# The residual as transposes at the head of an output projection's accumulation

## The reference

```python
x0  = adapter(x, cond)                      # low-rank, relu, plus x itself
h   = rmsnorm(x0) * norm1
q, k, v = split(h @ qkv_w + qkv_b)          # 16 heads, 4 key/value heads, 64 wide
q, k = rope(q), rope(k)
y   = attention(q, k, v, sink)              # causal, inside a sequence of 64
x2  = x0 + y @ proj_w + proj_b              # the residual and the output projection
h2  = rmsnorm(x2) * norm2
e, g = top4(h2 @ gate_w + gate_b)           # 4 of 32 experts, softmax of the four
out = x + x2 + sum_e g_e * (silu(h2 @ Wg_e) * (h2 @ Wu_e)) @ Wd_e
```

## Time and profile before

| what | value |
|---|---|
| median of three runs | 1031.28 us |
| lowest and highest run | 1029.86 and 1033.35 us |
| span of the profiled execution | 1031.5 us |
| its own time | the profile gives none beside the span |
| PE busy | 898.5 us, 87% |
| PE weight loads busy | 738.7 us, 72% |
| VectorE busy | 805.3 us, 78% |
| ScalarE busy | 512.2 us, 50% |
| GpSimd busy | 552.1 us, 54% |
| chain that ended last, PE's share | 49% |

### The profile page before, as it was taken

One profiled execution on the slowest core, in us unless ns is written; L12 is line 12 of the kernel. 1 busy time (PEld: TensorE's weight loads), 2 busy tenths in 40 slices (PEclk: granted clock), 3 DMA queues, 4 the chain that ended last, 5 costly groups with the idle time before them and its releaser, 6 DMA issues.

```text
span 1031.5 us, 21542 instructions
## 1 busy us (share of the span) xinstructions
PE 898.5 (87%) x7336; PEld 738.7 (72%) x7336; DVE 805.3 (78%) x1877; ACT 512.2 (50%) x1193; POOL 552.1 (54%) x513
## 2 busy tenths in 40 slices
PE   3859998988899989988871399999999999999986
PEld 1537676776677767766750288888888888888874
DVE  3878799988978898988857177777777777777787
ACT  1224362735437363453752266666666666566631
POOL 2436466877768688696768133333433344333340
PEclk9869999999999999999995599999999999999998
DMA  7235869687696977959875897778678758663599
GB/s 224 57 93 181 268 218 268 224 275 250 232 290 214 295 241 252 293 192 301 289 252 202 325 307 266 264 243 309 224 254 273 265 186 308 223 226 103 179 365 340
DMA packets 127684, 251.95 MB, mean 244 GB/s; under 512 B 18706, under 2 KB 66327, under 8 KB 127002
## 3 DMA queue, kind: packets, MB, share of 16 engines
q1 hardware_dynamic: 83866, 187.59, 55.4%
q0 software_dynamic: 13872, 34.64, 9.2%
q10 hardware_dynamic: 29840, 28.34, 9.0%
HBM read 136.19 MB, written 102.66 MB: 232 GB/s over the span
## 4 chain that ended last, share of the span: by engine, by line
PE 49%; POOL 14%; DMA 11%; DVE 10%; issue 7%; SPq 4%; ACT 3%; ACTq 0%; DVEq 0%; POOLq 0%
PE scores L970 10%; PE gbank L970 10%; POOL lists L672 10%; PE scores L989 5%; PE gbank L989 5%; DMA w_parts<-ring 4%; PE gbank L761 3%; DMA ring<-in_W_up 3%; POOL ring L679 3%; PE gbank L838 3%; DMA rows_in<-lists 3%; DVE ring L1401 2%; PE gbank L944 2%; PE scores L944 2%; PE gbank L979 2%
## 5 line engine op out<-in xcount | busy, mean ns | idle before, releaser
L694 POOL DMA_INDIRECT pick_rows<-rows_out,pair_i x161 | 160.9, 999 | 269.4 <-ACT rows_out L1232 260.7
L679 POOL TENSOR_TENSOR ring<-ring 128x512 fp32r<-128x512 f32 x96 | 122.6, 1291 | 47.0 <-ACT ring L1167 46.5
L970 PE MATMUL scores<-ring,in_part 128*128 x486 | 134.7, 412 | 0.0
L970 PE MATMUL gbank<-ring,in_part 128*128 x480 | 131.8, 409 | 0.0
L672 POOL DMA_INDIRECT lists<-put_rows,slot_i x104 | 103.4, 994 | 47.5 <-issue 28.0
L838 PE MATMUL gbank<-w_o,ring 128*128 128x256 f32 x512 | 123.2, 396 | 6.0 <-ACT ring L1113 6.0
L761 PE MATMUL gbank<-h_t,w_qk 128*128 128x512 f32 x480 | 122.1, 407 | 6.7 <-DVE h_t L1388 5.0
L1401 DVE SCALAR_TENSOR_TENSOR ring<-gbank,b_qk,rope 128x512 f32<-128x512 f32 x160 | 109.9, 745 | 16.6 <-PE gbank L761 16.0
L838 PEld LDWEIGHTS gbank<-w_o,ring 128*128 128x128 f32 x512 | 99.8, 199 | 26.0 <-ACT ring L1113 9.7
L761 PEld LDWEIGHTS gbank<-h_t,w_qk 128*128 128x128 f32 x480 | 89.7, 192 | 31.5 <-issue 8.6
L1167 ACT ACTIVATE ring<-ring 128x512 fp32r<-128x512 f32 x96 | 59.9, 628 | 90.8 <-DMA w_parts<-ring 50.9
(11 more groups left out here) (200 smaller groups left out, 1899.0 us busy)
## 6 DMA issues: line engine op xcount, KB each, us to landing
w_parts<-ring SPq DMA_DIRECT2D x192, 256.0 KB, 3.2
ring<-w_parts SPq DMA_DIRECT2D x32, 1536.0 KB, 7.9
rows_in<-lists ACTq DMA_DIRECT2D x161, 136.0 KB, 3.8
ring<-in_W_up SPq DMA_DIRECT2D x64, 256.0 KB, 4.0
picks<-pick_rows SPq DMA_DIRECT2D x8, 2048.0 KB, 12.8
ring<-in_W_down SPq DMA_DIRECT2D x32, 256.0 KB, 4.2
q_r<-rot SPq DMA_DIRECT2D x16, 512.0 KB, 6.9
q_r<-ring SPq DMA_DIRECT2D x16, 512.0 KB
```

The source lines that it names most:

```text
L679: e.tensor_tensor(lower, lower.bitcast(F32), upper.bitcast(F32), ALU.subtract).then_inc(s_lower, 1)
L694: e.indirect_dma_start(out=pick_rows, out_offset=bass.IndirectOffsetOnAxis(ap=pair_i[:, i:i + 1], axis=0), in_=rows_out[i % NY][:, :], in_ ...
L970: ins = e.matmul(front[i % FRONTS], in_parts[i % IN_BUFS][x][:, c, :], ring[:, bass.ds(at + y * WE + c * 2 * DFF, 2 * DFF)], start=k == 0, ...
```

## The change

The two blocks of the residual become transposes (`is_transpose`) and move ahead of the output products. The first of them begins the bank; the second and the eight products only add to it or write where nothing has been written. The wait for `x0_t` and the take of the bank come first, the wait for `y_t` moves behind the transposes, and the last product raises `s_proj`. Beside that, `plan_wait` becomes a table of 16-bit numbers.

```diff
+U16 = mybir.dt.uint16
...
-    plan_wait = sb("plan_wait", [1, 2 * P], I32)
+    plan_wait = sb("plan_wait", [1, 2 * P], U16)
...
         def project(t, banks):
             m, s = divmod(t, TPM)
-            w.wait_ge(s_y, 2 * t + 2)
             bank = take(banks[0])
-            for n in range(2 * REP):
-                e.matmul(bank[:, 0:D], y_t[:, n // REP, n % REP, :, :].rearrange("p b s -> p (b s)"), w_o[:, n, :],
-                         start=n == 0, stop=False)
             w.wait_ge(s_x0, KC * m + KC)
             for c in range(KC):
-                ins = e.matmul(bank[:, c * P:(c + 1) * P], x0_t[m % 2][:, c, s * P:(s + 1) * P], ident[:, :],
-                               start=False, stop=c == KC - 1)
+                e.matmul(bank[:, c * P:(c + 1) * P], x0_t[m % 2][:, c, s * P:(s + 1) * P], ident[:, :], is_transpose=True,
+                         start=c == 0, stop=False, skip_group_check=True)
+            w.wait_ge(s_y, 2 * t + 2)
+            for n in range(2 * REP):
+                ins = e.matmul(bank[:, 0:D], y_t[:, n // REP, n % REP, :, :].rearrange("p b s -> p (b s)"), w_o[:, n, :],
+                               start=False, stop=n == 2 * REP - 1, skip_group_check=True)
             ins.then_inc(s_proj, 1)
             freed[banks[0]] = (s_x2, t + 1)
```

## The result

Over 11 runs of each kernel on one chip the kernel before took 1032.66 us (1029.08 to 1037.07) and the changed kernel 1039.87 us (1036.12 to 1045.57). The ratio is **1.0072, with a 95% interval of 1.0054 to 1.0090**: slower by some 7 us, which is beyond the 0.3% that a measurement of this kernel can tell. The forecast of 1030.4 us with no change was wrong, and the range ended 6.6 us too low. The sentence about register loads that open gaps, last in the prediction's list of what would make it wrong, is the one that came true.

What follows compares the result with a forecast made beforehand. GpSimd's scatters and transfers were taken to bound the middle of the first stage, PE the expert tiles; 0.445 + 0.23 + 0.23 = 0.9 us off gave 1030.4 us, range 1027.0 to 1033.3.

Steps and rivals of the forecast that it cites:

- register loads that open gaps: Sign of a wrong prediction: PE's register loads would open gaps in PE between 590 and 986 us, in the expert tiles.
- the third part: 16-bit table of ready counts, loaded 21 times by PE's sequencer in the expert tiles: counted at 0, as PE's work covers it.
- Two transposes instead of four passes: Every projection's residual: transposes cost 0.218 us where products cost 0.445, so 0.227 us less PE work each, 7.3 over 32.
- the third rival: A transpose that opens a bank takes two passes, so only tile 29's hidden 0.445 us is left: 1030.8 us, chance 0.15.
- The order hides it before the last six tiles: Tiles 26 to 31: transposes fit into PE's idle time for y, 6.0 us in total, so the whole 0.445 comes off.
- Tile 28 gives nothing: Projection at 504.23 us: PE would come earlier and wait for VectorE's probabilities; gain 0, at most 0.2 us.
- Tile 29 passes its 0.445 us on through GpSimd: Projection at 513.52 us: all 0.445 us reach GpSimd's scatter at 523.07, whose last landing opens the expert stage.
- A term of 0.9 us: The forecast's whole gain on the path: 0.445 us from tile 29 and 0.23 each from tiles 17 and 4.
- the 0.23 us of tiles 4 and 17: First stage: tile 4 feeds query/key products VectorE waits for, tile 17 a tag in the middle; each passes 0.23 us.
- the first rival: PE holds the middle loop through VectorE, so every projection's 0.227 us counts: 1024.0 us, chance 0.2.
- The clock falls earlier: Close of the first stage: half clock before tile 31 gives 1034.4 us, with tile 30 as well 1037.9; chance 0.1.
- Expert tiles spaced as before: Sign of a right prediction: the spacing of the expert tiles, which hold no projection, stays unchanged.

Runs made afterwards that it cites:

- width alone: The kernel before with only the table of ready counts made 16 bits wide: 1039.37 us against 1034.53, ratio 1.0041; timed again, 1037.19 us, ratio 1.0046.
- Order alone: Against the kernel before: residual ahead of the wait for y but by ordinary products, counts in 32 bit and masked: 1034.46 us, ratio 1.0004.
- transposes behind the wait: Against the kernel before: residual by two transposes that begin the bank, but behind the wait for y, counts in 32 bit and masked: 1034.54 us, ratio 1.0011.

## Why the prediction was wrong

**The step that failed** is the price of the third part: "I count them at 0; if that cover were gone, it is 21 x 0.3 = 6 us of gain or 21 x 0.2 = 4 us of loss." Alone the 16-bit loads cost 4 to 5 us (ratios 1.0041 and 1.0046), and without their length the changed kernel was 5.7 us faster. Two things in the step were off, the size first.

*The size.* The bounds for a 16-bit load were the nearest rows, 271 and 792 ns. It took 1923 to 2420, in the median two and a half times the upper bound. Both rows were of 32-bit values and said nothing of width; with an operation in no row at all, a narrower type had no claim to be near them. A bound from a row of another type is a guess, and the range should have been left open above.

*The cover.* "PE has under 1 us of idle time in the 396 us where they run" is true, and shows only that the 0.59 us load was covered. It does not say by how much. The cover is the lead of the instruction stream: how much work PE still has in its queue when the load begins. The trace of before had it: from the start of a load to the next weight load of L989 it is 2.68 to 2.74 us at 12 of the 20 places, and at the other eight 0.93, 0.98, 1.03, 1.10, 1.46, 1.77, 1.78 and 1.97. A load of 2.0 us plus the 0.15 us behind it is late at these eight by 1.16, 1.11, 1.19, 1.19, 0.64, 0.47, 0.32 and 0.25 us (taking each load's own length after), **6.3 us together**. In the changed kernel the tiles at the 20 places took 6.2 us longer than their usual 2.53. So the size of the loss could have been estimated from the trace of before, had the load's length been known, and with that, its forecast would have been 1030.4 + 6.3 = 1036.7. That the two sums agree so closely is in part luck: the late places were ten in the changed kernel, two of them with a full lead in the trace of before, and the same sum over the tiles is 3.6 us in the second profile of the change and 5.8 and 5.2 in the two of width alone.

Where the lead was short, the stream had mostly just waited for a transfer. The step ahead of the load waits for the token rows of the tile after next. By the semaphores in the trace of before, these rows landed 0.55 to 0.59 us before the load began at six of the eight short places, and 0.92 us or more before it at all 14 others. The other two, with a lead of 1.77 and 1.78 us, are not settled. The landings differ from execution to execution, and so do the short places.

The rest, by the prediction's own steps:

- *Two transposes instead of four passes.* Right. In the middle of the opening, where PE does not wait, the pair starts at 96.24 and the products 0.21 us later; predicted was 0.218. The changed kernel's timeline of PE:

```profile
96.24 0.38 PE L839 MATMUL gbank<-ident,x_t 128*128 128x128 f32 x2
96.45 3.62 PE L843 MATMUL gbank<-w_o,ring 128*128 128x256 f32 x16
```

  That is also the end of the third rival: no transpose took two passes. The factor of four in the Trainium skill (TensorE: Matmul & The Clock Gate, Terms), which would put the pair at 0.11 us, does not agree with this row.

- *The order hides it before the last six tiles.* Right. The idle time ahead of the products fell from 6.0 us to 3.7, and ahead of the first projection below the pair fits wholly into the wait for y, whose second copy ends at 502.32 + 0.97 = 503.29 us. The closing of the first stage in the changed kernel, PE's timeline, then its chain:

```profile
502.86 0.44 PE L839 MATMUL gbank<-ident,x_t 128*128 128x128 f32 x2
503.35 3.72 PE L843 MATMUL gbank<-w_o,ring 128*128 128x256 f32 x16
507.36 1.09 PE L813 MATMUL gbank<-ident,prob 128*128 128x128 f32 x8 [0.29 <-DVE prob L1439]
...
511.62 0.44 PE L839 MATMUL gbank<-ident,x_t 128*128 128x128 f32 x2 [0.19 <-DVE glog L1458]
```

```profile
502.32 0.97 ACT ring L1114 x2
...
512.64 3.72 PE gbank L843 x16
```

- *Tile 28 gives nothing.* Right, and for the reason given: PE comes earlier to the transposes of probabilities and waits 0.29 us for VectorE, as the row at 507.36 shows.

- *Tile 29 passes its 0.445 us on through GpSimd.* Agrees. The scatter that began at 523.07 begins at 521.75, 1.3 us earlier (0.4 to 1.4 was expected), after the same idle time; the last is at 569.60 for 570.98. GpSimd's timeline in the changed kernel:

```profile
521.75 0.98 POOL L673 DMA_INDIRECT lists<-q_r,slot_i  x1 [2.77 <-ACT q_r L1160]
...
569.60 0.96 POOL L673 DMA_INDIRECT lists<-q_r,slot_i  x1 [0.30 <-issue]
```

  That it is the change's doing isn't shown: the expert stage begins anywhere between 580.3 and 587.7 us in the profiled executions, with the residual first by transposes (582.2, 583.1, 583.9, 587.4, 587.7) as without (580.3 to 585.1). Two of those five are later than all nine without, which five profiles don't settle. A term of 0.9 us lies below what one profile tells, the 0.23 us of tiles 4 and 17 all the more. No timing shows the 0.9 us either: the three kernels with the moved transposes and no long load stand at or above the kernel before.

- *PE's share of the middle stage is off the path* (the first rival, 1024.0 us, chance 0.2). Right. Order alone and transposes behind the wait gave 1.0004 and 1.0011, and the second of these, with a third of the residual's busy time gone, has an interval that ends at 0.9994, where the rival needs 0.993. The chain of the changed kernel from 166 to 494 us still belongs to GpSimd and the transfers, with 3.2% for PE's largest line:

```profile
by line: POOL lists L673 18.5%; issue 13.8%; DMA w_parts<-ring 12.3%; DMA ring<-in_W_up 10.6%; POOL ring L680 8.5%; SPq L542 3.8%; PE gbank L843 3.2%; SPq L509 2.2%; ACT ring L1168 2.1%; SPq L522 1.9%; PE gbank L762 1.7%; POOL ring L639 1.6
```

- *The clock falls earlier* (the second rival, 1034.4 to 1037.9 us). Wrong, though its time lies near the measured one. The granted clock is 1.00 from 505 us up to 539.87 and 0.50 from there to 591.07, after the products of tile 31 have ended at 532.15 + 3.72 = 535.87; and the loss is not in that stage. A rival that gives about the right time is not thereby the cause.

- *"Expert tiles spaced as before"* was the statement to look at first: they are not, and no part of the change that I had priced above zero touches them. The one part that does touch them was the one put at 0.

## What to carry to other kernels

A line of a diff that only narrows a type is a new operation if an engine's sequencer reads it: where no row shows that operation at that width, leave its price open above and ask what is behind it if it is several times as long. And "the engine is busy all through" covers a stall only up to the lead of its instruction stream; read that lead from the trace, at its shortest place, as the time from the start of the covered instruction to the next instruction that stands behind it. Here it was shortest where the stream had just waited for a transfer. Keep such tables in 32 bit, or split a long load: here 41 loads of 1 us cost nothing that could be told, and 21 of 2 us cost 4 to 5 us.

## What was not expected of the hardware

- PE's register load from SBUF took about 0.25 us for each value when the values had 16 bits: eight counts took 1.92 to 2.42 us, four 0.98 to 1.40 (median 0.99), while eight values of 32 bits took 0.59 in the median. Why the narrow values take longer isn't shown. The Trainium skill (DMA: Bandwidth & Descriptors, Latency and other measured facts) gives a `tensor_load` a floor of some 600 ns. The 0.59 us of PE's 32-bit load is near it, but SyncE's load of one value took 0.27, well under it, and that table does not tell of the width.
- The next weight load comes 0.15 us after a load that has used up the lead, at all ten places of the changed kernel where that happened.
- The granted clock between 166 and 494 us was 0.96 or 0.97 in all profiled kernels with transposes for the residual and 0.97 or 0.98 in the others. Whether that has to do with the 0 to 3 us left open wasn't tried.
